# Loads, stores and two small orders in the opening of a four-layer graph network kernel

## What is computed

```python
xn = _layernorm(x, axis=-1)                       # 3125 x 256
el = feat @ W_src + b_src                         # feat is xn
er = feat @ W_dst + b_dst
e = jax.nn.leaky_relu(el[src] + er[dst], NEG_SLOPE)
...
qkv = (x @ w_qkv + b_qkv).reshape(B, HW, HEADS, 3 * HEADC)
k = _ln(k, kln_g, kln_b)                          # over the 32 columns of a head
v = _ln(v, vln_g, vln_b)
kv = jnp.einsum('bhnd,bhne->bhde', k, v) / HW     # one 32 x 32 block per head
out = jnp.einsum('bhnd,bhde->bhne', q, kv)
```

## Time and profile before

| | |
|---|---|
| median of 3 runs | 9273.95 us (9271.48 to 9282.44) |
| the profiled execution | 9286.02 us |
| its span, first to last instruction | 9284.2 us |
| mean granted TensorE clock | 0.834 of full |
| busy share PE, DVE, ACT, POOL | 66%, 57%, 22%, 47% |

### The profile page before, as it was taken

How to read it: one execution, slowest core, us unless ns; L and a number is a source line. 1 busy time by engine, 2 the same in 40 slices (tenths; PEclk the granted TensorE clock), 3 DMA queues, 4 the chain that set the end, 5 groups by cost and what they waited for, 6 DMA issues and landing times. The chain is left out here.

```text
span 9284.2 us, 96347 instructions
## 1 busy us (share of the span) xinstructions
PE 6157.8 (66%) x28010; PEld 4815.4 (52%) x28010; DVE 5292.0 (57%) x14545; ACT 2033.5 (22%) x4839; POOL 4334.2 (47%) x4412
## 2 busy tenths in 40 slices
PE   0110369999967777775755555554965788886699
PEld 0110248888744466664533333343853677774466
DVE  7995579999845555553332222383114688887433
ACT  0000125555422100001120000022212333333322
POOL 0000036666667777776567777402020777771000
PEclk9999779999978888886867777775987777777799
DMA  0001023333301433332013333203860333331000
GB/s 21 0 0 28 10 84 97 97 97 97 78 11 42 119 105 105 105 105 55 8 24 105 105 105 105 75 1 107 305 218 23 98 98 98 98 98 34 12 14 21
DMA packets 405087, 698.69 MB, mean 75 GB/s; under 512 B 154168, under 2 KB 267809, under 8 KB 404071
## 3 DMA queue, kind: packets, MB, share of 16 engines
q0 software_dynamic: 206848, 480.28, 19.1%
q1 hardware_dynamic: 197726, 212.28, 7.2%
HBM read 633.06 MB, written 59.07 MB: 75 GB/s over the span
## 5 line engine op out<-in xcount | busy, mean ns | idle before, releaser
L735 POOL DMA_INDIRECT att_rows<-el_table,dst_order_row x1600 | 1564.1, 978 | 1198.8 <-POOLq L90 546.9
L712 PE MATMUL sum_sum<-sum_rows,sum_hot 128*125 128x256 f32 x3520 | 1218.0, 507 | 860.6 <-DMA sum_rows<-el_table,dst_order_row 464.9
L712 PEld LDWEIGHTS sum_sum<-sum_rows,sum_hot 128*125 128x125 f32 x3520 | 835.6, 249 | 1167.4 <-issue 810.0
L575 POOL DMA_INDIRECT dst_order_record<-records,dst_order_edge x784 | 811.0, 1034 | 403.1 <-issue 236.2
L640 POOL DMA_INDIRECT sum_rows<-el_table,dst_order_row x880 | 835.7, 950 | 295.1 <-issue 265.6
L640 POOL DMA_INDIRECT sum_rows<-rel_table,src_order_row x880 | 840.4, 955 | 274.9 <-issue 265.9
L662 DVE TENSOR_TENSOR gnn_acc<-gnn_acc,sum_sum 125x256 f32 x440 | 182.0, 414 | 1204.4 <-PE sum_sum L712 1200.4
L1216 PE MATMUL att_sum<-att_rows,att_hot 128*125 128x265 f32 x1440 | 474.5, 485 | 2.5 <-DVE att_rows L1107 2.4
L899 PE MATMUL att_sum<-att_rows,att_hot 128*125 128x257 f32 x1760 | 438.2, 391 | 0.0
L875 PE MATMUL att_found<-gnn_to_dst,att_hot_t 125*128 x1760 | 421.2, 382 | 0.5 <-issue 0.5
L939 ACT ACTIVATE att_rows<-att_rows,att_p 128x257 f32<-128x257 f32 x880 | 375.9, 499 | 7.1
(11 more groups left out here) (804 smaller groups left out, 13369.7 us busy)
## 6 DMA issues: line engine op xcount, KB each, us to landing
block_w<-in_L_ffn_W_dram SPq DMA_DIRECT2D x112, 512.0 KB, 6.3
block_w<-in_L_ffn_W_dram SPq DMA_DIRECT2D x56, 1024.0 KB
att_rows<-el_table,dst_order_row POOLq DMA_INDIRECT x1600, 2.8
rel_table<-open_st SPq DMA_DIRECT2D x25, 784.0 KB
sum_rows<-rel_table,src_order_row POOLq DMA_INDIRECT x880, 2.7
sum_rows<-el_table,dst_order_row POOLq DMA_INDIRECT x880, 2.7
dst_order_record<-records,dst_order_edge POOLq DMA_INDIRECT x784, 2.3
pairs<-zeros SPq DMA_DIRECT2D x1, 7168.0 KB
```

The lines of the kernel that those rows point to most:

```text
L575: nc.gpsimd.indirect_dma_start(o["record"][:, k, :], None, o["records"], bass.IndirectOffsetOnAxis(ap=o["edge"][:, k:k + 1], axis=0)).then ...
L712: last = nc.tensor.matmul(slot(u), hot[u % HOTS_S][:, g, :], rows[l][:, g, :], start=(g == 0), stop=(g == G - 1))
L735: nc.gpsimd.indirect_dma_start(rows[l][:, g, 0:width], None, table, bass.IndirectOffsetOnAxis(ap=o["row"][:, k:k + 1], axis=0)).then_inc(s ...
```

## The change

1. build_sorts gets an SP block, which issues the load of x and open0's 17 weight loads (now from a function weights0) when the sorts begin. A short phase "open0_in" behind dst_tiles waits for them; "x_in" is gone.
2. The four source lists are stored from SP within the dst_tiles phase (build_unit_tiles gets `to_dram`), which waits for them before it ends.
3. To make room, the six key buffers of the sorts lie in XNT, `place` of build_run_shares lies in a key buffer, and open0's `sq` lies in a buffer of the edge records.
4. build_open, in all its nine uses: xT is gone, ACT copies `wide` straight into XNT with one instruction, and the multiplies read XNT.
5. open0 and open2 get kv_late: norm no longer waits for kv, and PE does kv(i-1) behind multiply(i), and the last kv at the end. (open0's last two then stand next to each other.)
6. open0's `st` gets two buffers, so that take_units(i) waits for post and kv of i-2.

```diff
@@ build_sorts(nc, c, streams, landed, pairs)
+        @block.sync
+        def _(sp):
+            for to, frm in pairs:
+                sp.dma_start(to, frm).then_inc(landed, 16)
+
@@ build_unit_tiles(nc, c, tag, o, to_dram=())
+            @block.sync
+            def _(sp):
+                for to, frm in to_dram:
+                    sp.dma_start(to, frm).then_inc(s["stored"], 16)
+                if to_dram:
+                    sp.wait_ge(s["stored"], 16 * len(to_dram))
@@ build_open, norm of DVE
-                        if kv:
+                        if kv and not kv_late:
                             dve.wait_ge(s["kv_added"], i - 1)
@@ build_open, prepare of ACT
                     act.wait_ge(s["flipped"], i + 1)
-                    if i >= 2:
-                        act.wait_ge(s["unit"], NUG // per * (i - 1))
-                    a.copy(xT[l][:].rearrange("p k (j x) -> p (k j) x", x=R), turned(wide[:])).then_inc(s["xt_ready"], 1)
-                    act.wait_ge(s["xt_ready"], i + 1)
-                    a.copy(XNT[:, :, i * GN:(i + 1) * GN], xT[l][:]).then_inc(s["xnt_ready"], 1)
+                    a.copy(XNT[:, :, i * GN:(i + 1) * GN].rearrange("p k (j x) -> p k j x", x=R), turned(wide[:]).rearrange("p (k j) x -> p k j x", k=KB)).then_inc(s["xt_ready"], 1)
@@ build_open, PE
+                def add_kv(i):
+                    pe.wait_ge(s["post"], i + 1)
+                    kv(t, kv_p, bufs[i % 2]).then_inc(s["kv_added"], 1)
+
                 turn(0)
                 for i in range(GROUPS):
                     if i + 1 < GROUPS:
                         turn(i + 1)
                     multiply(i)
-                    if kv:
-                        pe.wait_ge(s["post"], i + 1)
-                        kv(t, kv_p, bufs[i % 2]).then_inc(s["kv_added"], 1)
+                    if kv and not kv_late:
+                        add_kv(i)
+                    elif kv and i:
+                        add_kv(i - 1)
+                if kv_late:
+                    add_kv(GROUPS - 1)
@@ open0
-    build_open(... hand=(ACT.Sqrt,), st_lanes=1, pair=True)
+    build_open(... hand=(ACT.Sqrt,), pair=True, kv_late=True)
@@ open2
-    build_open(... hand=(ACT.Exp,), pool_work=pool_work)
+    build_open(... hand=(ACT.Exp,), pool_work=pool_work, kv_late=True)
@@ the opening
-            order_edges(nc, c, I, by_src, by_dst)
-            put_in(nc, "x_in", [(m["X"][rows], by_tile(I["x"])[rows]) for rows in (slice(0, EVEN), slice(EVEN, R))] + [(dram["src_" + n], by_src[n][:]) for n in ("node", "row", "w", "tile")])
-        layer0(nc, c, m, I, dram, by_dst)
+            landed = nc.alloc_semaphore("open0_landed")
+            flat = m["XNT"][:].rearrange("p k n -> p (k n)")
+                order_edges(nc, c, I, by_src, by_dst, [flat[:, k * ROWS_A:(k + 1) * ROWS_A] for k in range(6)], landed, pairs,
+                            [(dram["src_" + n], by_src[n][:]) for n in ("node", "row", "w", "tile")])
+            wait_in(nc, "open0_in", landed, len(pairs))
+            layer0(nc, c, m, I, dram, by_dst, to_dst, first, weights)
```

More of the change, by code:

```diff
@@ L191, in up_part, with build_sorts @@
     return in_fours(ap, 1 << (turn // 2))[:, :, 0::3, :]
-def build_sorts(nc, c, streams):
+def build_sorts(nc, c, streams, landed, pairs):
     blocks = ROWS_A // P
@@ L311, in _, with build_run_shares @@
                                       turned[:].rearrange("p (b n) -> p n b", b=blocks)[:, 0:CHUNKS_S // blocks, :]).then_inc(s["moved"], 1)
-def build_run_shares(nc, c, keys, shift, weight):
+def build_run_shares(nc, c, keys, shift, weight, place):
     L = 512
@@ L321, in build_run_shares @@
         sb = lambda n, sh, d=F32: ctx.enter_context(nc.sbuf_tensor(f"runs_{n}", sh, d))
-        run, place, new, end = (sb(n, [P, ROWS_A]) for n in ("run", "place", "new", "end"))
+        run, new, end = (sb(n, [P, ROWS_A]) for n in ("run", "new", "end"))
         run_i, place_i = end[:].bitcast(I32), place[:].bitcast(I32)
@@ L1399, in store_rows, with build_open @@
     eng.dma_start(to[EVEN:R], frm[EVEN:R]).then_inc(sem, 16)
-def build_open(nc, c, layer, X, XN, XNT, loads, units, post, stores, kv, kv_cols, hand=(), pool_work=None, post_reads_units=True, st_lanes=2, tile_store=None, pool_with=None, ahead=None, pair=False):
+def build_open(nc, c, layer, X, XN, XNT, loads, units, post, stores, kv, kv_cols, hand=(), pool_work=None, post_reads_units=True, st_lanes=2, tile_store=None, pool_with=None, ahead=None, pair=False, kv_late=False):
     tag = f"open{layer}"
@@ L1695, in kv @@
         return last
-    build_open(nc, c, 0, m["X"], m["XN"], m["XNT"], loads, units, post, stores, kv, keep_blocks(c, 1.0 / NODES, m["KV"]), hand=(ACT.Sqrt,), st_lanes=1, pair=True)
+    build_open(nc, c, 0, m["X"], m["XN"], m["XNT"], loads, units, post, stores, kv, keep_blocks(c, 1.0 / NODES, m["KV"]), hand=(ACT.Sqrt,), pair=True, kv_late=True)
 def open1(nc, c, m, I, dram, pool_work):
@@ L1768, in kv @@
         return last
-    build_open(nc, c, 2, m["X"], m["XN"], m["XNT"], loads, units, post, stores, kv, keep_blocks(c, 1.0, m["KV"], ones=True), hand=(ACT.Exp,), pool_work=pool_work)
+    build_open(nc, c, 2, m["X"], m["XN"], m["XNT"], loads, units, post, stores, kv, keep_blocks(c, 1.0, m["KV"], ones=True), hand=(ACT.Exp,), pool_work=pool_work, kv_late=True)
 def open3(nc, c, m, I, dram):
@@ L2991, in alloc_order, with order_edges @@
     return o
[L2994 removed]
+def order_edges(nc, c, I, by_src, by_dst, keys, landed, pairs, to_dram):
     build_constants(nc, c)
     store_records(nc, c, I, by_dst["records"])
[L2998 to L2999 removed]
+    orders = [order_by_pair(nc, c, I, by_dst, keys[0:2], to_dram), order_by_src(nc, c, I, by_src, [keys[2], keys[3], keys[4]]), order_by_edge(nc, c, I, by_dst, keys[4:6])]
+    build_sorts(nc, c, [next(order) for order in orders], landed, pairs)
     for order in reversed(orders):
```

94 lines of the change are left out of this document (47 added, 47 removed).

## The result

The changed kernel takes 9178.2 us in the median of four runs (9171.9 to 9182.7), the kernel before 9274.5 beside it: a ratio of 0.9895, with a 95% interval of 0.9883 to 0.9906, which is 97 us (87 to 109) less. The forecast was 9165 with a range of 9150 to 9187, so the time lies inside the range, 13 us above the forecast. The profiled execution took 9182.7 against 9286.0, 103.3 less.

The account below looks back on a forecast made before the run. DVE bounds the sorts, transfers alone fill 83 us before open0, where DVE and PE mostly take turns. Savings of 81.6 + 1.1 + 5.7 + 3.5 + 17.2 = 109.1 take the median from 9273.95 to 9164.9 us, range 9150 to 9187.

Parts of the forecast that it names:

- The loading gap: Between dst_tiles and open0's norm: loads and stores moved under earlier work make the norm begin 81.6 us sooner.
- Its covers: Sorts (652 us) hide loads of at most 82.5 us, dst_tiles (37 us) the stores; without the latter, up to 20.3 back.
- Keys in XNT and traffic: In the sorts: new key addresses and transfers beside DVE cost nothing; booked at nothing.
- rival D: Sorts get slower through XNT and transfers; decides from 0.108 us per instruction, at 0.138 the median is 9305; chance 0.03.
- The second copy: On ACT before the square root: dropping it saves 1.1 us in open0 and 5.7 in five other stages.
- The product out of the norm's way: In open0: 5.3 us of DVE waits gained, 1.8 lost to the clock; 3.5 saved.
- The last group: In open0, group 4's multiplies no longer wait for group 3's product; 17.2 us saved, 19 all warm, 9 all cold.
- open2: The late product there gains nothing because POOL sets the end; up to 18.5 us if POOL were no bound.
- rival C: open2 gains too, as POOL's issues might depend on PE and DVE; up to 18.5 + 3.4 us more; chance 0.09.
- The whole: Over the whole kernel: all savings sum to 109.1 us, median 9164.9; chance of the forecast as summed 0.66.

Follow-up runs that it names:

- the seventh experiment: Changed kernel with x loaded forty more times during the sorts, one after another; 9245.1 us, run once.
- the second profile of before: The kernel before, run once more without any edit; 9295.2 us, run once.
- the fourth experiment: Changed kernel with open0's products of groups 0 to 2 ahead of the turn, DVE not waiting for them; 9164.0 us, run once.
- the eleventh experiment: Changed kernel with norms first in open0, open2g, open3, open3g, 38 records moved out of open2, its products 0 to 2 ahead of the turn; 9011.1 us, 0.9712.
- the second profile: The changed kernel run and compared again without any edit; 9173.7 us in the median, 0.9888 against the kernel before.
- the ninth experiment: Changed kernel with 38 of open2's 134 edge records gathered in the layer normalisation ahead of it; 0.9857 against the kernel before.
- tenth experiments: Changed kernel with the 38 records moved, but open2's product back ahead of the next turn and DVE waiting; 0.9878 against the kernel before.

## Why the prediction was right, and where its terms were off

*The loading gap*, 81.6 forecast, 81.7 and 81.5 measured. Its covers were measured too: without the sorts' cover 44.6 come back, without that of the stores 6.1, which the prediction had bounded at 20.3.

*Keys in XNT and traffic* (rival D), booked at nothing: 692 ns before and after, and also with the queues at 0.84 for the whole stretch. D was priced to decide at 0.108 us per instruction; the rows show no difference at a resolution of 0.001. The Trainium skill ("SBUF — State Buffer", on the two physically separate sides) says that transfers can't slow an engine's access; the seventh experiment agrees, with 692 ns at a share of 0.84.

*The second copy*, 1.1 each: 1.27 in open0 (group 1's reciprocal gained that over group 0's start). In open0g, open2g and open3g the waits for the root went from 3.7 to 2.4, and in open1g from 2.9 to 1.6. These four stages became 2.3, 1.0, 1.3 and 0.8 shorter (table, first profile), 5.4 together, against 5.7 booked for five stages. The fifth, open3, shows nothing: it was 0.7 and 0.4 longer in the changed kernel's two profiles, and 2.4 longer in the second profile of before. The copy into XNT takes 1.20 us, as the first one did.

*The product out of the norm's way*, 3.5 forecast: the distance from group 0's post-processing to group 3's shrank by 3.64 us. The parts agree too: 5.3 of waits came off, and the three distances from turn to post-processing grew from 64.4 to 66.1 together, 1.7 against the 1.8 forecast. Singly they changed by -0.3, +0.7 and +1.2, so that the 22.03 of the forecast, read from one turn, fits their mean and none of them; that it fits so well is partly luck. What the fourth experiment shows is that I compared two states that were both partly cold. I set "no product ahead" against "product ahead", 22.03 against 21.42, and took 0.6 for the price of a cold array. That 21.42 had a granted clock of 0.92, because the norm waited for the product and the array stood idle for 2.12 us before the turn. At the full clock throughout it is 19.80. Against that order the late product costs 1.4, 2.4 and 2.9 us in the three groups, and dropping only the wait would have gained some 7 us more.

The Trainium skill ("TensorE: Matmul & The Clock Gate", Part 1: The HAM clock gate) says that an idle array runs at half the clock until it has worked for a while. The trace of open0 agrees in kind (a turn of 2.35 us after idle time, of 1.29 behind the product); open2 in the eleventh experiment shows 8.7 us of products that didn't bring the full clock back, and why isn't shown. The prediction applied the rule to the turn alone, and the multiplies behind the turn pay about half of it (3.5 of the 6.7 us).

*The last group*, 17.2 forecast, 16.4 measured (17.1 in the second profile). The three remaining pairs started at 1114.20, 0.95 after the hand-over, as the prediction had it; the first of them took 6.4 us (3.78 and 2.95, overlapping) in place of a warm 3.4, where I had added 2 for the cold start.

*open2*, booked at nothing: nothing. The ninth and tenth experiments show that POOL hid the gain. What rival C supposed, that POOL ends earlier when PE and DVE do, was false; its price for a stage without that bound, 18.5, was too low, since it left out the last group (some 34 by PE's last matmul).

*The whole.* The touched stages gave 81.7 + 21.0 + 5.4 = 108.1 in the first profile and 109.5 in the second (table), where the prediction said 109.1. The medians gave 96 and 100. What lies between isn't an effect that a run has shown. The profiled execution of before was itself 12 us above its median, and the long untouched stages differ by several us between profiles of the same kernel. The attention behind open0 was 1.2 us longer on the mean of the twelve profiles of changed kernels, and the same to 0.1 in the two of before; whether that is chance stays open, and the rest as well. The interval of the second comparison holds the forecast saving, that of the first ends at its edge (0.9883 against the 0.9882 that 109.1 would make).

## What to carry to other kernels

Where an engine-bound stretch has empty queues, the next stage's loads belong there, whole and early; the gain here was the time that the loads used to stand alone, and it could be read off one idle time (83.33, less two phase boundaries).

A gain on an engine that isn't last in its stage is only a loan: in open2 34 us lay unused, and 27 of them showed once records were moved off POOL. Look who ends the stage before and after.

If two engines take turns, ask first which instruction stands in whose queue: moving the norms ahead of all post-processing gave 67 us, where trimming the waits in the same loop had given 21. And a small piece of work directly ahead of a chain on TensorE may be worth more than its own time, or less: in open0 the 4 us product ahead of the turn gained some 7 us over the late one, in open2 the 8.7 us product lost 5.8. It has to be tried in each stage.

## What the runs showed of the hardware

The granted clock's price in an alternating loop, for the same turn and multiplies in open0: 19.7 to 19.8 us right behind 4 us of products (granted clock 1.00), 21.4 to 21.5 with 2.1 us of idle time between (0.92), and 21.2 to 22.8 after 37 to 39 us of idle time (0.93 to 0.87 in the first profile). In the last case the three turns of one profile differ by up to 1.5 us from each other.

DVE's compare instruction in the sorts took 692 ns with the DMA engines 84% busy, writing into the same memory, and 692 ns with no transfer.

From one gather of a record on POOL to the next it was 1.25 us in open2's plain stretches, but 55 / 38 = 1.45 on average in the normalisation. The intervals there aren't all longer. Beside DVE's batch statistics and normalising steps they are 1.25; the long ones, 1.5 to 2.2 us and three in each group, stand beside the three DVE instructions that combine two tensors (125x1280, L2445 to L2447), as in the ninth experiment's timeline:

```profile
4477.63 0.95 POOL L582 DMA_INDIRECT dst_order_record<-records,dst_order_edge  x1 [0.30 <-issue]
4478.44 1.49 DVE L2445 TENSOR_TENSOR norm_t<-norm_t,norm_gamma 125x1280 f32<-125x1280 f32 x1
4478.88 1.86 POOL L582 DMA_INDIRECT dst_order_record<-records,dst_order_edge  x1 [0.30 <-issue]
4479.97 1.49 DVE L2446 TENSOR_TENSOR norm_t<-norm_t,norm_beta 125x1280 f32<-125x1280 f32 x1
4481.05 1.23 POOL L582 DMA_INDIRECT dst_order_record<-records,dst_order_edge  x1 [0.30 <-issue]
```

The normalising step (L1387) took 428 ns there in place of 410, the batch statistics 413 against 414. What they share wasn't tried.
